# An edge sort with 96 of each merged 128 keys kept: rows of 1536 keys in place of 2048, three-way steps, and the first phase's order filled anew

## The reference, cut to what matters

```python
x = x + L0_gnn(layernorm(x), adj)          # aggregate over adj, PReLU
x = x + L0_ffn(layernorm(x))               # 6 experts, top 2
x = x + L1_gnn(layernorm(x), adj)          # convolution, distances, GRU
x = x + L1_ffn(layernorm(x), edge_index)   # below
x = x + L2_gnn(...); x = x + L2_ffn(...); x = x + L3_gnn(...); x = x + L3_ffn(...)

def L1_ffn(x, edge_index):                 # M = 8192 nodes
    h = (x @ W_gat).reshape(M, 4, 4)       # 4 heads, 4 experts
    src = concat([edge_index[0], arange(M)]); dst = concat([edge_index[1], arange(M)])
    e = leaky_relu(a_src[src] + a_dst[dst], 0.2)
    alpha = softmax of e over the edges that share dst
    agg = segment_sum(h[src] * alpha, dst) + b_gat
    scores = layernorm(agg).reshape(M, 4, 4).mean(1)
    w, i = softmax(top_2(scores))          # then 4 experts with gelu, weighted by w
```

## Time and profile before

| | |
|---|---|
| median of 3 runs | 2918.04 us (2912.92 to 2920.19) |
| profiled execution, its span | 2906.4 us; no other time of it is shown |
| mean granted TensorE clock | 0.885 |
| PE busy | 2279.4 us, 78% of the span |
| DVE busy | 1857.1 us, 64% |
| ACT busy | 1379.7 us, 47% |
| POOL busy | 1327.1 us, 46% |
| sort's merge operations (line 1628) | 356 operations |

### The profile page before, as it was taken

The page is one execution under the profiler, slowest core; times in us unless marked ns, Lnnn a source line. Parts: engine busy times, 40 slices in busy tenths (PEclk is TensorE's granted clock), DMA queues, the critical chain, the costliest instruction groups (busy, mean ns, idle before and its releaser), DMA issues. The chain is left out here.

```text
span 2906.4 us, 41877 instructions
## 1 busy us (share of the span) xinstructions
PE 2279.4 (78%) x12152; PEld 1686.0 (58%) x12152; DVE 1857.1 (64%) x4712; ACT 1379.7 (47%) x3040; POOL 1327.1 (46%) x1219
## 2 busy tenths in 40 slices
PE   4888898989888879888821717579999998999990
PEld 3444444545545445555511616568888888888980
DVE  5988998776978847433367674377465476665312
ACT  3544556555646354455521506355646534444540
POOL 1020111010101066646765667723745747767776
PEclk9998999989898979899965758789999998998995
DMA  4010101000100111422213223233636536565762
GB/s 148 1 38 1 31 1 31 5 27 1 31 11 20 26 38 29 138 74 77 75 34 116 57 69 104 45 100 113 178 85 160 161 80 187 136 159 137 189 157 75
DMA packets 282475, 228.42 MB, mean 79 GB/s; under 512 B 90029, under 2 KB 234399, under 8 KB 281330
## 3 DMA queue, kind: packets, MB, share of 16 engines
q1 hardware_dynamic: 247442, 179.50, 21.1%
q0 software_dynamic: 34784, 46.03, 7.9%
HBM read 162.95 MB, written 63.70 MB: 78 GB/s over the span
## 5 line engine op out<-in xcount | busy, mean ns | idle before, releaser
L983 POOL TENSOR_TENSOR a_rstd<-a_var,minus_half 128x4 f32<-128x4 f32 x64 | 120.8, 1888 | 911.9 <-DVE a_var L1537 904.4
L1628 DVE TENSOR_TENSOR room<-room 128x1024 f32<-128x1024 f32 (+1 forms) x356 | 489.9, 1392 | 23.2 <-ACT room L1379 13.3
L2160 POOL DMA_INDIRECT c_slots<-sent,c_tokens_of_slots x340 | 354.9, 1044 | 197.1 <-PE bank L2331 100.6
L2425 ACT ACTIVATE weights_f<-bank,c_expert_b 128x256 f32<-128x256 f32 x680 | 276.8, 470 | 190.3 <-PE bank L2206 190.0
L2206 PE MATMUL bank<-c_experts_w,weights_f 128*128 x2720 | 345.2, 282 | 18.8 <-ACT weights_f L2425 11.6
L2206 PEld LDWEIGHTS bank<-c_experts_w,weights_f 128*128 128x128 f32 x2720 | 336.9, 198 | 30.6 <-issue 26.4
L2206 PE MATMUL bank<-c_slots_t,c_expert_w 128*128 128x256 f32 x1360 | 342.4, 397 | 12.2 <-ACT weights_f L2425 6.0
L2206 PEld LDWEIGHTS bank<-c_slots_t,c_expert_w 128*128 128x128 f32 x1360 | 255.6, 198 | 48.9 <-issue 16.7
L1013 PE MATMUL bank<-a_h1p,weights_a 128*128 128x512 f32 x544 | 249.8, 608 | 2.8 <-ACT a_dist_exp L1356 2.8
L2622 DVE TENSOR_TENSOR c_made<-bank,c_expert_b 128x256 f32<-128x256 f32 x170 | 72.1, 424 | 261.1 <-PE bank L2206 241.4
L80 POOL DMA_INDIRECT got_room<-table_dram,own_rows x184 | 191.5, 1041 | 75.4 <-issue 75.4
(11 more groups left out here) (529 smaller groups left out, 4563.7 us busy)
## 6 DMA issues: line engine op xcount, KB each, us to landing
c_expert_w<-in_weights_c SPq DMA_DIRECT2D x170, 256.0 KB
made<-c_made SPq DMA_DIRECT2D x170, 128.0 KB
results_dram<-a_results SPq DMA_DIRECT2D x64, 256.0 KB
room<-results_dram SPq DMA_DIRECT2D x16, 1024.0 KB, 7.4
c_expert_b<-in_f_b SPq DMA_DIRECT2D x170, 64.0 KB
room<-in_adj SPq DMA_DIRECT2D x32, 256.0 KB
sent<-c_rows_to_send SPq DMA_DIRECT2D x32, 256.0 KB, 3.8
c_slots<-sent,c_tokens_of_slots POOLq DMA_INDIRECT x340
```

The costliest lines, as they stand in the source:

```text
L983: rstd.did(g_.tensor_tensor(st.rstd[:, :], st.var[:, :], env.minus_half[:, 0:GT], ALU.pow), what, k)
L1628: v.tensor_tensor((dv[:, :, 0, :], other(dv))[j], sv[:, :, 0, :], other(sv), (ALU.min, ALU.max)[j]).then_inc(sort_step, 1)
L2160: pool.indirect_dma_start(out=XS[p.r % S_BUFS][:, j, :], out_offset=None, in_=env.sent_dram[p.q], in_offset=bass.IndirectOffsetOnAxis(ap=T ...
L2425: go(H[p.m % 2][:, c, :], U[c // 2][:, (c % 2) * SLOT:(c % 2 + 1) * SLOT], func, bias=bias).then_inc(hidden, 1)
```

## The change

After the cut and the steps that sort its blocks again ("mid", rows of `PER_MID` = 2048), a new "trim" merges blocks of 128 in pairs and takes the 96 smallest of each: rows of 1536 keys. From there lengths are 96 times a power of two, and a merge of three parts is done in three steps, `third_0` to `third_2`, each a minimum and a maximum on a third of the row, with the far end of the target buffer as scratch. `env.left_out` is joined by a second test at the trim. Turned columns hold 12 blocks in place of 16. `PREFER_A` has new numbers throughout, and three tasks of later groups ("l0out", "c1", "se") now need that of group 0, whose instructions hold the waits for the weights. `PREFER_C`, the order of the second phase, is not touched. In the diff the table is cut to three of its lines.

```diff
--- before.py
+++ after.py
@@ -39,7 +39,9 @@
 PER_IN = E_TOTAL // P
 BLOCK_BITS = 7
 KEPT_BITS = BLOCK_BITS - 1
-PER = PER_IN >> (BLOCK_BITS - KEPT_BITS)
+PER_MID = PER_IN >> (BLOCK_BITS - KEPT_BITS)
+BLOCK, TRIMMED = 1 << BLOCK_BITS, 96
+PER = PER_MID // BLOCK * TRIMMED
 KEY_ROWS = P * PER // SLOTS
 HALVES = 2
 HALF = NT // HALVES
@@ -439,8 +441,6 @@
 TURNS = GROUPS // STREAMS
 
 N0 = EXPERTS0
-ROWBITS = PER.bit_length() - 1
-ALLBITS = (P * PER).bit_length() - 1
 NBLK = PER // P
 FILL = 4
 FILLS = NBLK // FILL
@@ -463,44 +463,45 @@
 def sort_plan():
 
 
-    climb = lambda k: [(k - 1, True)] + [(b, False) for b in range(k - 2, -1, -1)]
-    phases = [("wide", [e for k in range(1, BLOCK_BITS + 1) for e in climb(k)], None)]
-    phases.append(("cut", [(KEPT_BITS, True)], None))
-    phases.append(("row", climb(KEPT_BITS + 1)[1:] + [e for k in range(KEPT_BITS + 2, ROWBITS) for e in climb(k)], None))
-    phases.append(("flip", None, 0))
-    phases.append(("row", climb(ROWBITS), None))
-    for k in range(ROWBITS + 1, ALLBITS + 1):
-        phases.append(("flip", None, k - ROWBITS))
-        phases.append(("to_column", None, None))
-        phases.append(("column", [(b - ROWBITS, False) for b in range(k - 1, ROWBITS - 1, -1)] + [(b, False) for b in range(ROWBITS - 1, 6, -1)], None))
-        phases.append(("to_row", None, None))
-        phases.append(("row", [(b, False) for b in range(6, -1, -1)], None))
+    falls = lambda l: [("row", (1 << b, False)) for b in range(l.bit_length() - 2, -1, -1)]
+    thirds = lambda l: [(f"third_{part}", (l, False)) for part in range(3)]
+    climb = lambda l: [("wide", (l, True))] + [("wide", (1 << b, False)) for b in range(l.bit_length() - 2, -1, -1)]
+    merge = lambda kind, l: [(kind, (l, True))] + thirds(l // 3) + falls(l // 3)
+    phases = [e for k in range(BLOCK_BITS) for e in climb(1 << k)]
+    phases += [("cut", (1 << KEPT_BITS, True))] + [("mid", step) for kind, step in falls(1 << KEPT_BITS)]
+    phases += merge("trim", TRIMMED)
+    l = 2 * TRIMMED
+    while l < PER // 2:
+        phases += merge("row", l)
+        l *= 2
+    phases += [("flip", 0)] + merge("row", l)
+    for k in range(1, P.bit_length()):
+        phases += [("flip", k), ("to_column", None)]
+        phases += [("row", (1 << b, False)) for b in range(k - 1, -1, -1)]
+        phases += thirds(PER // 3) + [("row", (c * P, False)) for c in (2, 1)]
+        phases += [("to_row", None)] + falls(P)
     steps, cur = [], 0
-    for kind, exchanges, bit in phases:
-        for exchange in exchanges or [None]:
-            steps.append((kind, exchange, bit, cur))
-            cur ^= 1
+    for kind, step in phases:
+        steps.append((kind, step, cur))
+        cur ^= kind not in ("third_0", "third_1")
     turning = ("to_column", "to_row")
     units, fills, last_of = [], [], {}
 
-    def unit(n, k, cols, due):
-        kind, step, bit, at = steps[n]
-        for j in range(1 if step is None else 2):
-            units.append(Unit(n, k, j, j + 1, kind, step, bit, at, cols, due))
-        last_of[n, k] = len(units) - 1
-
-    n = 0
-    while n < len(steps):
-        kind, step, bit, at = steps[n]
+    def unit(n, due):
+        kind, step, at = steps[n]
+        cols = slice(0, {"wide": PER_IN, "mid": PER_MID, "cut": PER_MID}.get(kind, PER))
+        if kind == "flip":
+            units.append(Unit(n, 0, 0, 1, kind, None, step, at, cols, due))
+        else:
+            units.extend(Unit(n, 0, j, j + 1, kind, step, None, at, cols, due) for j in range(2))
+        last_of[n] = len(units) - 1
+
+    for n, (kind, step, at) in enumerate(steps):
         if kind in turning:
             for c0 in range(0, NBLK, FILL):
-                fills.append(Fill(kind, bit, at, c0, last_of[n - 1, 0]))
-            n += 1
-            continue
-        turned = n > 0 and steps[n - 1][0] in turning
-        due = len(fills) if turned else 0
-        unit(n, 0, slice(0, PER_IN if kind == "wide" else PER), due)
-        n += 1
+                fills.append(Fill(kind, None, at, c0, last_of[n - 1]))
+        else:
+            unit(n, len(fills) if n > 0 and steps[n - 1][0] in turning else 0)
     return units, fills, cur
 
 
@@ -531,19 +532,21 @@
 HOP = 0.15
 WHOLE = ("begin", "gates")
 PREFER_A = {
-    "adjT": (45.0, 63.0), "att": (9.0, 45.0), "begin": (-111.0, 44.0), "c1": (-41.0, 107.0), "c2": (-28.0, 18.0), "clear": (-52.0, -137.0),
...
+    "adjT": (381.0, 2249.0), "att": (1804.0, 2794.0), "begin": (-1409.0, -295.0), "c1": (-340.0, 80.0), "c2": (-662.0, -1503.0),
...
+    "sort": (-875.0, 1999.0), "stats0": (2737.0, -126.0), "stats1": (225.0, 1115.0), "stats2": (7.0, 1559.0), "stats3": (2737.0, -1797.0),
...
 
 
@@ -563,7 +566,7 @@
         "adjT": lambda g: [("loada", g)] + back("xt3", g - 2),
         "stats0": lambda g: [("load", g)] + back("norm3", g - 2),
         "l0agg": lambda g: [("norm0", g), ("adjT", g)],
-        "l0out": lambda g: [("l0agg", g), ("prepare", 0)] + back("hh", g - 2),
+        "l0out": lambda g: [("l0agg", g), ("prepare", 0)] + back("hh", g - 2) + back("l0out", min(g, 1) - 1),
         "stats1": lambda g: [("l0out", g), ("norm0", g)],
         "xt1": lambda g: [("norm1", g), ("l0agg", g)],
         "lg": lambda g: [("rh", g)],
@@ -591,8 +594,8 @@
         "gt": lambda g: [("gate3", g)],
         "gb": lambda g: [("gt", g)],
         "stats2": lambda g: [("gb", g), ("comb", N0 * g + N0 - 1)],
-        "c1": lambda g: [("xt2", g)],
-        "se": lambda g: [("xt2", g), ("fold", 0)] + back("keep", g - 2),
+        "c1": lambda g: [("xt2", g)] + back("c1", min(g, 1) - 1),
+        "se": lambda g: [("xt2", g), ("fold", 0)] + back("keep", g - 2) + back("se", min(g, 1) - 1),
         "dist": lambda g: [("se", g), ("c1", g)],
         "att": lambda g: [("dist", g)],
         "msg": lambda g: [("se", g)],
@@ -740,7 +743,7 @@
 
 
 def sort_long(unit):
-    wide = unit.cols.stop - unit.cols.start
+    wide = 2 * PER // 3 if unit.kind.startswith("third") else unit.cols.stop - unit.cols.start
     return [(DVE, 0.1 + wide * (0.00056 if unit.step is None else 0.00053))]
 
 
@@ -1617,12 +1620,26 @@
                     v.tensor_scalar(dst[:, u.cols], src[:, u.cols], env.sign[:, u.bit:u.bit + 1], None, ALU.mult).then_inc(sort_step, 1)
                     return
                 if u.kind == "cut" and u.first == 0:
-                    link(v.tensor_reduce(env.left_out[:, :], src[:, 1 << KEPT_BITS::1 << BLOCK_BITS], AX.X, ALU.min))
+                    link(v.tensor_reduce(env.left_out[:, :], src[:, 1 << KEPT_BITS:PER_IN:BLOCK], AX.X, ALU.min))
+                if u.kind == "trim" and u.first == 0:
+                    link(v.tensor_reduce(env.spill[:, :], src[:, TRIMMED:PER_MID:BLOCK], AX.X, ALU.min))
+                    link(v.tensor_tensor(env.left_out[:, :], env.left_out[:, :], env.spill[:, :], ALU.min))
                     link(v.tensor_scalar(env.left_out[:, :], env.left_out[:, :], env.tail_i[:, 0:1].bitcast(F32), None, ALU.is_lt))
-                b, mirrored = u.step
-                pairs = lambda t, cols, gap: t[:, cols].rearrange("p (h x l) -> p h x l", x=2, l=gap)[:, :, :, 0:1 << b]
-                sv = pairs(src, slice(0, PER_IN), 1 << BLOCK_BITS) if u.kind == "cut" else pairs(src, u.cols, 1 << b)
-                dv = pairs(dst, u.cols, 1 << b)
+                l, mirrored = u.step
+                split = lambda t, n, x: t.rearrange("p (h x l) -> p h x l", x=x, l=n)
+                if u.kind.startswith("third"):
+                    (a, b, c), (low, mid, high) = ([split(t[:, u.cols], l, 3)[:, :, k, :] for k in range(3)] for t in (src, dst))
+                    lower, upper, rest = (split(dst[:, PER + k * PER // 3:PER + (k + 1) * PER // 3], l, 1)[:, :, 0, :] for k in range(3))
+                    outs, ins = {"third_0": ((lower, upper), (a, b)), "third_1": ((low, rest), (lower, c)), "third_2": ((mid, high), (rest, upper))}[u.kind]
+                    v.tensor_tensor(outs[u.first], *ins, (ALU.min, ALU.max)[u.first]).then_inc(sort_step, 1)
+                    return
+                sv, dv = src[:, u.cols], split(dst[:, u.cols], l, 2)
+                if u.kind == "cut":
+                    sv = split(src[:, 0:PER_IN], BLOCK, 2)[:, :, :, 0:l]
+                elif u.kind == "trim":
+                    sv = split(src[:, 0:PER_MID], BLOCK, 2)[:, :, :, 0:l]
+                else:
+                    sv = split(sv, l, 2)
                 other = lambda t: t[:, :, 1, ::-1] if mirrored else t[:, :, 1, :]
                 for j in range(u.first, u.last):
                     v.tensor_tensor((dv[:, :, 0, :], other(dv))[j], sv[:, :, 0, :], other(sv), (ALU.min, ALU.max)[j]).then_inc(sort_step, 1)
```

More of the change, by code:

```diff
@@ L533 @@
 PREFER_A = {
-    "adjT": (45.0, 63.0), "att": (9.0, 45.0), "begin": (-111.0, 44.0), "c1": (-41.0, 107.0), "c2": (-28.0, 18.0), "clear": (-52.0, -137.0),
-    "comb": (-11.0, -36.0), "count": (-34.0, 30.0), "cv": (-45.0, -28.0), "dist": (130.0, -30.0), "edge": (60.0, 45.0), "encode": (41.0, -21.0),
```

(13 more changed lines are left out.)

## The result

The changed kernel takes 2809.94 us (median of 4 runs, 2807.43 to 2810.89) against 2915.48 us for the kernel before on the same chip (4 runs, 2910.50 to 2920.19): ratio 0.965, 95% interval 0.9633 to 0.9666, so 105.5 us less.

What follows compares the result with a forecast made beforehand. Before the first edge gather TensorE (86.1% busy) and VectorE (79.8%) wait for each other, neither full. That stretch was to give -50 us, the rest 0: 2906.4 to 2856, plus 11.6 for the median, 2868 us; range 2815 to 2925.

Steps and rivals of the forecast that it cites:

- Operations and durations: Sort's merge operations on VectorE: counts by shape times measured durations, 422.8 us, -72.8; VectorE in all -77 us, to 845.
- One reading of the slices: Opening look at the profile's time slices: TensorE called nearly empty in slices 20 to 24; no size attached.
- Behind the hand-over: After the first edge gather at 1206 us: gathers 272 us, gates 51, second phase 1377, all taken as unchanged, 0.
- The slope: Stretch before the first edge gather: TensorE's share rises 0.46 point per point less on VectorE; length 1119 us, -37.
- the term for the refilled order: Stretch before the first edge gather: new preferences share VectorE out again, so -50 us taken, between -37 and -97.
- A second term: TensorE's busy time before the first edge gather: fewer fills and counting matmuls bring 995.1 us to 985.
- VectorE is the bound: Rival: the stretch before the first edge gather shrinks with VectorE's work, -97 us, 2821 us; chance 0.14.
- TensorE-bound: Rival: TensorE and its latencies set the stretch before the first edge gather, -12 us, 2906 us; chance 0.18.
- The new order loses more: Rival: merge steps go ahead of statistics and shifts, delaying the last group's stored rows; +25 us, 2943 us; chance 0.12.
- The power on GpSimd: Normalisation's power on GpSimd: some 40 of 64 shorten by 0.27 us beside shorter merges, 11 us, counted inside the -50.

Runs made afterwards that it cites:

- e1: Changed kernel (new sort) with the old preference table PREFER_A; 2875.3 us, ratio 0.9886 to the kernel before.
- e12: New sort with its short merges, run in the order searched for 234 lengthened merge operations; 2852.0 us, ratio 0.9792 to the kernel before.
- e2: Kernel before, old sort, with the new PREFER_A and the three new needs; 2960.4 us, ratio 1.0173.
- e7: Kernel before, old sort, with the three new needs and its own newly searched table; 2880.9 us, ratio 0.9903.
- e8: Changed kernel with a third table, searched starting from the old one; 2834.3 us, ratio 0.9740 to the kernel before.
- e9: Changed kernel with a fourth table, searched further from its own new one; 2805.4 us, ratio 0.9634 to the kernel before.
- e4: Changed kernel in its own order with 112 matmuls issued twice, 73.6 us more TensorE work; 2866.2 us, ratio 0.9845 to the kernel before.
- e6: Kernel before in its own order with 112 matmuls issued twice, 76.6 us more TensorE work; 2967.2 us, ratio 1.0204.
- e11: Changed kernel with 112 matmuls issued twice and a table searched anew for them; 2866.2 us, ratio 0.9841 to the kernel before.

## Why the prediction was wrong, point by point

*Operations and durations* were right. Count times mean is 56 x 2.290 + 14 x 1.224 + 242 x 0.956 + 66 x 0.689 = 422.2 us against 422.8 forecast; VectorE in the stretch 843.6 against 845; 168 transposes in 42 fills, 48 counting matmuls. One reading of the slices was loose: slices 20 to 24, called nearly empty for TensorE, have the digits 8, 2, 1, 7 and 1; nothing in the sum rests on it.

*Behind the hand-over* was right: 265.5, 52 and 1384 us against 272, 51 and 1377 forecast, each within 10.

*The slope* was about right for what it describes. It gave 37 us for an order that stays fitted to the old lengths; e1 gave 34 us in the median (45 at the edge), e12 gave 22 for four fifths of the dose. Put into the same formula, e1's own busy times (971.2 and 847.1) give a stretch of 1108 us, and 1110.6 was measured. It was right by luck in part: it tied TensorE's share to VectorE's, and the first halves of e1 and e2 show that the tie is not fixed.

*The step that failed* is the term for the refilled order, "I take -50, nearer to the slope". It left the refilled order 13 us beyond the slope. In its place the runs show 55 us at the edge (1160.6 in e1, 1105.5 in the changed kernel, which differ in the table alone), and 2.4% of the time, 0.9886 less 0.9650, which is 69 us of 2909. A second term was off beside it: TensorE's work was put at 985 us and measured 955.9. With the measured 955.9 and 843.6 the formula of the slope gives 1094 us where the forecast had 1119, and the stretch is 1055.5; so TensorE's term is worth 25 of the 50 us missed, and the refilled order gave 39 us beyond the slope in place of 13. VectorE's share was also expected to fall to about 76%, and it stayed at 79.9%.

Part of the table's gain is not the change's at all: e7 shows 29 us for a better table on the old sort, the three new needs included. Set against e7's, the new sort with tables of its own is 47 (e8), 71 (the changed kernel) and 76 us (e9) faster, for 78 to 82 us of VectorE's work and 12 to 20 of TensorE's between their stretches. So what I should have asked was not where between two share bounds the stretch lies but what each chain to the hand-over gains. The sort chain held 73 us of removed merge operations and had 86 us to give; the group chain had to receive it from the order.

*VectorE is the bound* (2821 us) gave the nearest number, and VectorE's share, 79.9%, is the one on which that rival rests. It is still not the mechanism: e1 has the same VectorE work and 2875 us, and e4 makes TensorE's work cost 0.82. By the Trainium skill (Perfetto Trace Analysis, Identifying the Most-Contended Engine) TensorE's headroom is judged by its weight loads or by its share of the peak arithmetic. The weight loads are busy 52% of the changed kernel's stretch (548.9 of 1055.5). e4 and e6 disagree with reading headroom from that here: the added matmuls did not disappear into it, and in e11, whose order was filled for them, they still cost 61 us against e9.

*TensorE-bound* (2906) fell with the result: TensorE did not keep its 86.1%, its share rose to 90.6%. *The new order loses more* (2943) is what e2 did on the old sort, but not at the place I named: its groups ran ahead and the sort came late.

*The power on GpSimd* gained more than I put in: before it took 1.888 us in the mean of 64, after 1.534, 23 us in all against 11; it is inside the stretch and was not tested alone.

```profile
L983 POOL TENSOR_TENSOR a_rstd<-a_var,minus_half 128x4 f32<-128x4 f32 x64 | 120.8, 1888 | 911.9 <-DVE a_var L1537 904.4
...
L986 POOL TENSOR_TENSOR a_rstd<-a_var,minus_half 128x4 f32<-128x4 f32 x64 | 98.2, 1534 | 829.4 <-DVE a_var L1540 822.0
```

*What stays open.* Which of the groups' tasks the new table moves to effect was not separated, nor were the 14 saved fills on TensorE, nor the three new needs, which no run has without a new sort or a new table. TensorE's busy time fell by 39 us to 955.9 where 985 was forecast: 13 us are transposes and counting matmuls, 6 are matmuls of layer 1's experts that now run behind the hand-over, and about 20 are the same matmuls in less time, at a mean granted clock of 0.93 against 0.91. e1, with the same sort, has 971.2 at 0.92. Why the same matmuls take less time was not tested. Between tables of one sort lie 25 us and more that no run here explains.

## What to carry to other kernels

Where two engines work through fixed lists and wait for each other, the busy shares of a stretch do not say what a saving is worth: added work cost 0.63 to 0.88 us for each, removed work gave back 0.36 with its order kept and 0.45 (34 for 75, in the median of e1; 0.60 at its edge) with its table kept, and 47 to 76 us for about 80 once the table was searched anew. So forecast the chains that meet at the end of the stretch one by one, and give a refilled order its own term, with the gain that the old code would have from refilling in it. And a share that comes out unchanged is no proof of a bound: double the work of the other engine and look.
